# Two reorderings in an attention block's instruction order: the LayerNorm step starts four work units later, and ScalarE takes an exponential before an output copy

## The reference, cut to what matters

```python
mod = (_silu(c) @ wmod).reshape(B, 6, 1, -1)          # shift, scale and gate, twice
h = _layernorm(x) * (1 + ca) + sa
x = x + ga * attention(h)        # 16 query heads in 4 groups, 4 K/V heads, D = 128, causal softmax, out projection
h = _layernorm(x) * (1 + cb) + sb
x = x + gb * ffn(h)              # Hadamard, up and gate (1024), silu, Hadamard, down
```

## Time and profile before

| what | value |
| --- | --- |
| median of 3 runs | 955.19 us (954.87 to 955.91) |
| the profiled execution, its own time | 955.91 us |
| its span, first to last instruction | 954.1 us |
| granted TensorE clock, mean | 1.000 |
| TensorE busy | 917.7 us, 96% of the span |
| VectorE busy | 664.6 us, 70% |
| ScalarE busy | 506.6 us, 53% |
| GpSimd busy | 509.9 us, 53% |

### The profile page before, as it was taken

The page is one execution under the profiler, slowest core; times in us unless marked ns, Lnnn a source line. Parts: engine busy times, 40 slices in busy tenths (PEclk is TensorE's granted clock), DMA queues, the critical chain, the costliest instruction groups (busy, mean ns, idle before and its releaser), DMA issues.

```text
span 954.1 us, 14771 instructions
## 1 busy us (share of the span) xinstructions
PE 917.7 (96%) x5236; PEld 790.5 (83%) x5236; DVE 664.6 (70%) x1364; ACT 506.6 (53%) x1062; POOL 509.9 (53%) x647
## 2 busy tenths in 40 slices
PE   5999999999999999999999999999999998999997
PEld 4878888888888888888888888888888886888887
DVE  5687758776787578757875787578757776874555
ACT  3366556665666566646664666466646664321111
POOL 1387628762887188718871887188718674120000
PEclk9999999999999999999999999999999999999999
DMA  7005200520043004300430043003300221000000
GB/s 273 1 23 166 67 1 27 159 70 1 23 148 85 1 23 143 89 1 23 141 93 1 23 138 96 1 23 101 99 1 23 83 84 45 1 4 19 22 22 23
DMA packets 41284, 56.42 MB, mean 59 GB/s; under 512 B 4736, under 2 KB 31616, under 8 KB 41088
## 3 DMA queue, kind: packets, MB, share of 16 engines
q1 hardware_dynamic: 40496, 55.33, 18.3%
q10 hardware_dynamic: 720, 0.21, 0.1%
HBM read 35.86 MB, written 19.66 MB: 58 GB/s over the span
## 4 chain that ended last, share of the span: by engine, by line
PE 62%; DVE 19%; ACT 11%; POOL 3%; issue 3%; DMA 2%; SPq 0%; DVEq 0%; POOLq 0%; ACTq 0%
PE ps L1133 15%; PE ps L1135 15%; PE ps L1134 15%; DVE ps L1027 7%; ACT prob L758 6%; PE ps L1260 4%; PE ps L1245 4%; DVE pt_lo L1031 4%; PE ps L1251 4%; PE ps L1248 4%; DVE blocks L1008 2%; ACT pt_hi L783 2%; ACT o_hi L793 1%; POOL prob L646 1%; DVE pt_lo L1000 1%
## 5 line engine op out<-in xcount | busy, mean ns | idle before, releaser
L758 ACT ACTIVATE prob<-ps,nmax 128x1024 f32<-128x1024 f32 (+7 forms) x256 | 190.0, 743 | 179.4 <-DVE nmax L1027 178.8
L643 POOL TENSOR_TENSOR rinv<-rsum,mone 128x1 f32<-128x1 f32 x256 | 150.8, 589 | 209.2 <-ACT prob L758 208.1
L646 POOL TENSOR_SCALAR prob<-prob,rinv 128x1024 f32<-128x1024 f32 (+7 forms) x256 | 191.5, 748 | 53.1 <-POOL rinv L643 53.1
L1027 DVE CUSTOM_DVE_ANT_0 ps<-ps,mask_f 128x1024 f32<-128x1024 f32 (+7 forms) x256 | 192.0, 757 | 25.5 <-PE ps L1251 24.9
L1031 DVE TENSOR_TENSOR pt_lo<-ps,pt_hi 128x512 fp32r<-128x512 f32 x221 | 151.8, 688 | 51.8 <-ACT pt_hi L783 50.8
L783 ACT ACTIVATE pt_hi<-ps 128x512 fp32r<-128x512 f32 x221 | 130.7, 595 | 40.4 <-PE ps L1260 39.5
L1260 PE MATMUL ps<-ident,prob 128*128 128x128 f32 x884 | 132.8, 274 | 6.8 <-ACT h L723 4.3
L1133 PE MATMUL ps<-pt_hi,v_hi 128*128 128x512 f32 x288 | 129.7, 450 | 0.3 <-DVE pt_lo L1031 0.2
L1260 PEld LDWEIGHTS ps<-ident,prob 128*128 128x128 f32 x884 | 106.4, 140 | 25.5 <-ACT h L723 6.4
L1245 PE MATMUL ps<-k_hi,q_hi 128*128 128x512 f32 (+4 forms) x384 | 114.1, 351 | 6.4 <-ACT prob L758 6.4
L1134 PE MATMUL ps<-pt_lo,v_hi 128*128 128x512 f32 x288 | 113.5, 394 | 0.0
(11 more groups left out here) (139 smaller groups left out, 1825.1 us busy)
## 6 DMA issues: line engine op xcount, KB each, us to landing
spill<-blocks SPq DMA_DIRECT2D x16, 512.0 KB, 3.0
raw_down<-spill SPq DMA_DIRECT2D x64, 128.0 KB, 3.3
w_raw<-in_wqkv SPq DMA_DIRECT2D x8, 768.0 KB, 6.5
spill<-blocks SPq DMA_DIRECT2D x14, 384.0 KB, 2.6
raw_down<-spill SPq DMA_DIRECT2D x56, 96.0 KB, 2.6
wp_raw<-in_wproj SPq DMA_DIRECT2D x8, 512.0 KB, 4.4
spill<-blocks SPq DMA_DIRECT2D x14, 256.0 KB, 2.4
raw_down<-spill SPq DMA_DIRECT2D x56, 64.0 KB, 2.1
```

Source lines behind the costliest of these rows:

```text
L643: g_.tensor_tensor(rinv[:, at, h:h + 1], rsum[:, at, h:h + 1], mone[:, :], ALU.pow).then_inc(rinv_done, 1)
L646: g_.tensor_scalar(row(i, h), row(i, h), rinv[:, at, h:h + 1], 1.0, ALU.mult, ALU.mult).then_inc(prob_done, 1)
L758: a_.activation(row(i, h).rearrange("p (a n) -> p a n", a=nb), score_banks(i, h).rearrange("p (a n) -> p a n", a=nb)[:, :, 0:w], ACT.Exp, ...
L1027: v_.tensor_tensor_reduce(scores, scores, late, -1.0, 3.0e38, ALU.add, ALU.min, nmax[:, place(n), h:h + 1]).then_inc(max_done, 1)
```

## The change

The first two edits move the five parts of the LayerNorm step in the list: `LF` from unit 9 to unit 13 and `LN` from unit 11 to unit 15 (windows are counted from their own first unit, so 0 and 2 become 4 and 6), and `L`, `LH`, `LL` from units 18, 19, 20 to 19, 20, 21. The third edit swaps two statements in ScalarE's program: at a `V` step that both ends a block and has `moved(t, n + LAG)`, `exps()` comes before the copy to o_hi, not after it. Such steps are V13 (in every turn) and V24 (in all but the last).

```diff
             if p == 1:
-                for k, what in ((0, "LF"), (2, "LN")):
+                for k, what in ((4, "LF"), (6, "LN")):
                     fill[k].append((t, what, 0, 0))
             if p == 2:
-                for k, what in ((0, "L"), (1, "LH"), (2, "LL")):
+                for k, what in ((1, "L"), (2, "LH"), (3, "LL")):
                     fill[k].append((t, what, 0, 0))
...
                     a_.activation(by_head(pt_hi, n), swapped_tile(n), ACT.Copy).then_inc(eh_done, 1)
                     exps()
+                if what == "V" and moved(t, n + LAG):
+                    exps()
                 if what == "V" and n == LAST[UNITS[n][0]]:
                     i = UNITS[n][0]
                     act.wait_ge(pv_done, this(pv_done, t, n + 1))
                     a_.activation(heads(o_hi[:, out_slot(i), :]), by_heads(O[i]), ACT.Copy).then_inc(oh_done, 1)
-                if what == "V" and moved(t, n + LAG):
-                    exps()
```

## The result

The changed kernel takes 962.97 us (median of 6 runs, 960.52 to 966.28) against 954.85 us (6 runs, 954.48 to 955.91): ratio 1.0083, 95% interval 1.0062 to 1.0103. Its runs spread over 5.8 us where those of before spread over 1.4. The profiled execution took 962.86 us, its span 961.1.

What follows compares the result with a forecast made beforehand. TensorE, busy 917.7 of 954.1 us, was taken to bound the kernel, so only its stalls count. Added 7.8 + 1.5 + 0.4 = 9.7 us gave 965.6, or 964.9 for the median; range 962 to 968, with rival (a) 959.5 to 969.

Steps and rivals of the forecast that it cites:

- LF: LayerNorm statistics on VectorE, moved to unit 13: 1.24 us, of which 0.5 us fills idle time.
- E15: Step of moved unit 15; its low part, a VectorE subtraction ahead of S2.0's maximum, starts 0.74 us later, at 372.59.
- LN: LayerNorm step on VectorE, moved to unit 15 ahead of o_lo, where VectorE idles 0.81 us: cost 0, at most 0.64.
- the swap at V24: Exponential ahead of o_hi at the start of window 3, which TensorE's chunks fill: cost 0, at most 0.56 us.
- The swap at V13: ScalarE's exponential of S2.1 goes ahead of o_hi of block 1, making o_hi 0.56 us later on top.
- Y1: TensorE's step waiting for o_lo of block 1: starts 0.74 + 0.56 = 1.30 us later.
- what stands behind o_lo: On VectorE, X5.2, a low part and the maxima of S2.2 and S2.3 all go with o_lo, 0.56 us in full.
- E17: Step of moved unit 17; its low part, a VectorE subtraction behind o_lo and X5.2, moves with o_lo, 0.56 us in full.
- L and S4.3: TensorE's stall at T19 becomes about 1 us at the LayerNorm transpose L; S4.3 is late by S2.3's exponential's delay, 1.30 us.
- The sum: Whole kernel: turns 1 to 6 at 1.30 us each, 7.8, plus 1.5 and 0.4 for the end turns, 9.7 us.
- rival (e): Longer TensorE stalls drop its clock, losing some 3 us a turn: 24 us, 989 us; chance 0.01.
- The rule weighed: VectorE two-SBUF-input and GpSimd operations lock each other out; set aside, since the trace shows 0.15 us, ending at 377.60, not 378.2.

Runs made afterwards that it cites:

- e1: Kernel before with only the third edit, the exponential ahead of the copy to o_hi at V13 and V24: 954.81 us against 954.67, ratio 1.0001.
- e7: Kernel before with GpSimd's low-part subtractions cut to 8 of 64 columns of each group: 945.74 us, ratio 0.9903.
- e4: Kernel before with only the second edit, L, LH and LL one unit later: 954.21 us, ratio 0.9998.
- e9: Kernel before with VectorE taking row maxima ahead of the low-part subtractions of units 15, 17 and 25: 943.54 us, ratio 0.9883.
- e8: Kernel before with L moved behind Y6 (unit 22), LH to unit 24, LL to unit 25; LF and LN stay: 955.85 us, ratio 1.0012.

## Why the prediction was right, and where it was not

The number and the sign were right. The sum behind it was not.

**LF.** Forecast: E15's low part starts 0.74 us later. From S5.3's maximum it is 377.25 - 373.79 = 3.46 us instead of 2.66: 0.80. Right for the start. But it then took 0.88 and not 1.11 us, so S2.0's maximum was 0.58 late.

**LN, and the swap at V24.** Forecast 0. LN now ends at 380.20 and o_lo starts at 380.97, behind 0.77 us of idle time, so LN holds up nothing there. The swap at V24 is a part of e1, which costs nothing. Right, though neither has a run of its own.

**The swap at V13, and Y1.** o_hi is 1.13 us late, 0.56 of it the exponential; Y1 starts 381.72 - 373.79 = 7.93 us after the maximum instead of 6.80: 1.13, forecast 1.30. Right, as far as Y1.

**The step that failed** is what stands behind o_lo: that X5.2, E17's low part and the maxima "all go with it". E17's low part started 1.13 us late and ended 0.52 late (382.72 - 373.79 = 8.93, before 8.41), since what I had booked as its duration, 1.26 us, was 0.65 of work and the rest waiting for GpSimd. That is also why the swap costs nothing by itself (e1), and most of why taking the wait out of the old kernel was worth 9 us (e7).

**L and S4.3.** That S4.3 is late by what S2.3's exponential is late held exactly: 0.53 us (384.24 - 373.79 = 10.45, before 9.92) and 0.53 (17.95, before 17.42). Only the amount was 1.30 in my sum. L's wait was 0.29 us, not 1, for the same reason. e4 shows the exchange of one wait for the other with nothing else in it.

**The sum** of 7.8 us for turns 1 to 6 is 2.0 us of the new order in truth (6 x 0.34), where these turns are 6.3 us longer together. Of the rest, 3 us are rival (e), which I gave a chance of 0.01: the clock fell behind Y1 in 3 of these 6 turns (4 of all 8), at 1.0 us each, not 3. The last 1.2 us are in turns 1 and 3, with the late transfer and the lost race. Turn 0 is 1.9 us longer where I said 1.5, with a drop and a late transfer in it, and turn 7 is 0.4 shorter where I said 0.4 longer. So two errors met: a term 1 us too large in each turn, and mechanisms left out that cost nearly as much in every second turn. That the total came within 1.9 us is luck.

**The rule weighed.** I set the Trainium skill's "SBUF — State Buffer" (Who interferes with whom) aside: "the trace disagrees". It was my reading that was wrong. The rule has VectorE stand until 377.06, and 377.06 plus 0.65 is 377.71, where the trace has 377.60; I had added 1.11, a duration that held such a wait itself. Rows 10 had the answer, 0.69 us for the same instruction with no GpSimd subtraction beside it, and I used that row only for its idle time. Of the 30 such subtractions of before, 22 took over 1 us. All of these began while a GpSimd subtraction or scaling ran, and all ended 0.54 to 0.55 us after it did. The 7 in window 3, with no GpSimd instruction beside them, took 0.69 each, and so did the one of rows 10, beside a 128x1 power. The rows fit the rule but for 0.1 us.

**The clock.** By the Trainium skill, "TensorE: Matmul & The Clock Gate", idleness of TensorE throttles its clock. The rows here agree: 0.50 behind stalls of 1.88 us and more in some turns and not in others, 1.00 in every turn once the stall is filled.

## What to carry to other kernels

Before a duration goes into a sum, look for the same instruction elsewhere in the trace: if VectorE's two-tensor subtraction is 0.69 us in one place and 1.26 in another, the difference is a wait in disguise, and moving the instruction moves its end by less than its start. A stall of TensorE of about 2 us has a price beyond its length when the clock falls behind it; a spread of the runs that grows with a change is the first sign, though late transfers and a lost race spread them too. Put first what others wait for (a row maximum) and behind it what may stand still for another engine and has slack (a low part): that order was worth 1.2% here (e9), where the change of this document cost 0.8%.

## What the runs showed of the hardware that was not expected

- VectorE's subtraction of two SBUF tensors (128x512) took 0.64 to 0.69 us with no GpSimd subtraction or scaling under way. Begun while a GpSimd subtraction or scaling ran, it ended 0.53 to 0.55 us after that one did, in all 196 cases of over 0.72 us in 13 profiles (0.76 to 1.60 us long); the recorded duration holds the wait. The other way round, GpSimd's 1.30 became 1.72 when VectorE had started 0.32 us earlier (e9).
- With starts within 0.1 us of each other either engine can win: VectorE 1.26 and GpSimd 0.80 us in one turn, 0.69 and 1.35 in the next.
- The granted clock stood at 0.50 for 3.4 us each time it fell. The fall came 0.3 to 1.6 us after TensorE had resumed (the changed kernel, two profiles), and in e8 0.2 us before; each drop cost 1.0 us here.
- Up to 8 matmuls a turn that nobody reads, in a stall, made a kernel 2.8 us faster (961.79 to 958.99).
